# A graph kernel's passages between stages without a barrier, weights on another queue, and attention endings in six steps

## What is computed

```
h = relu(layernorm(x))
for W_r, W_sl, W_el in two layers:                       # "layer one", "layer two"
    self_msg = where(in_deg == 0, h @ W_el, h @ W_sl)
    agg = segment_sum((rel_embed[type] + h[src]) @ W_r, dst)
    h = rrelu(agg * deg ** -0.5 + self_msg)
x = x + h                                                # x2
h3 = relu(layernorm(x))
qk = h3 @ Wqk + bqk ;  v = h3 @ Wv + bv                  # attention over the same edges
e = exp(clip(qk[dst] . qk[src] / sqrt(D), -5, 5) - max)
out = segment_sum(e / sum(e) * v[src], dst) @ Wo + bo
x = x + gamma * layernorm(out + h3) + beta
```

## Time and profile before

| | us |
|---|---|
| median of 3 runs | 870.51 (868.87 to 872.46) |
| the profiled execution | 870.01 |
| its span, first to last instruction | 868.3 |
| PE busy | 732.6 (84%) |
| DVE busy | 527.7 (61%) |
| ACT busy | 431.5 (50%) |
| POOL busy | 245.1 (28%) |

### The profile page before, as it was taken

One profiled execution on the slowest core, in us unless ns is written; L12 is line 12 of the kernel. 1 busy time (PEld: TensorE's weight loads), 2 busy tenths in 40 slices (PEclk: granted clock), 3 DMA queues, 4 the chain that ended last, 5 costly groups with the idle time before them and its releaser, 6 DMA issues. The chain is left out here.

```text
span 868.3 us, 15380 instructions
## 1 busy us (share of the span) xinstructions
PE 732.6 (84%) x5767; PEld 545.2 (63%) x5767; DVE 527.7 (61%) x931; ACT 431.5 (50%) x1085; POOL 245.1 (28%) x273
## 2 busy tenths in 40 slices
PE   4266698898889898977399999859999999999993
PEld 3255587788778788866289999824444444444463
DVE  4987997786768677541033333414476767666676
ACT  0445765564555555551011111237767676767661
POOL 6130010000001111100000000026666666666662
PEclk9999799799989999987699999979999999999996
DMA  4100200033300000011311111130000000000000
GB/s 130 33 1 18 59 2 7 23 103 71 100 9 7 8 8 7 8 60 61 108 31 37 36 37 37 37 106 1 1 4 21 3 22 2 24 0 24 2 25 18
DMA packets 39763, 27.89 MB, mean 32 GB/s; under 512 B 5311, under 2 KB 38163, under 8 KB 39686
## 3 DMA queue, kind: packets, MB, share of 16 engines
q1 hardware_dynamic: 39206, 26.35, 10.5%
q10 hardware_dynamic: 480, 0.53, 0.2%
HBM read 13.28 MB, written 10.80 MB: 28 GB/s over the span
## 5 line engine op out<-in xcount | busy, mean ns | idle before, releaser
L1462 POOL TENSOR_TENSOR counts<-counts,work 125x500 f32<-125x500 f32 x150 | 162.3, 1082 | 97.5 <-DVE work L1526 84.1
L1016 PE MATMUL sums<-work 125*128 125x196 f16 (+15 forms) x1220 | 157.1, 256 | 24.7 <-DVE work L825 24.6
L1384 PE MATMUL a_ps_o<-work 125*128 125x500 f32 (+1 forms) x350 | 159.2, 545 | 7.1 <-DVE work L1530 6.7
L1526 DVE SCALAR_TENSOR_TENSOR work<-a_ps_s,counts 125x500 f32<-125x500 f32 x150 | 101.6, 677 | 93.5 <-ACT a_ps_s L1482 93.4
L1372 PE MATMUL a_ps_s<-work 128*125 128x500 f32 x300 | 152.0, 589 | 6.9 <-PEq L534 6.9
L819 DVE TENSOR_TENSOR work<-work,counts 125x3024 f16<-125x3024 f16 (+1 forms) x60 | 114.3, 1906 | 65.5 <-PE sums L1018 62.4
L1477 ACT ACTIVATE a_ps_s<-a_ps_s,work 125x500 f32<-125x500 f32 (+1 forms) x157 | 102.1, 650 | 86.5 <-PE a_ps_s L1372 83.4
L1018 PE MATMUL sums<-work 125*128 125x10 f16 (+15 forms) x800 | 133.7, 196 | 0.0
L1187 ACT CAST counts<-sums 128x364 f32 (+38 forms) x305 | 131.9, 472 | 2.1 <-issue 1.4
L977 PE MATMUL sums<-counts 125*128 125x250 f16 (+1 forms) x975 | 124.5, 275 | 10.0 <-ACT work L1129 10.0
L825 DVE TENSOR_TENSOR work<-work,counts 125x4200 f16<-125x4200 f16 (+15 forms) x120 | 125.5, 1086 | 0.0
(11 more groups left out here) (178 smaller groups left out, 703.3 us busy)
## 6 DMA issues: line engine op xcount, KB each, us to landing
first_columns<-counts SPq DMA_DIRECT2D x5, 610.4 KB
counts<-first_columns SPq DMA_DIRECT2D x5, 610.4 KB
counts<-counts SPq DMA_DIRECT2D x5, 468.8 KB
counts<-in_x SPq DMA_DIRECT2D x5, 312.5 KB
h_nodes<-counts SPq DMA_DIRECT2D x5, 312.5 KB
work<-in_x SPq DMA_DIRECT2D x12, 125.0 KB
x_after_messages<-work SPq DMA_DIRECT2D x12, 125.0 KB
h_attention<-work SPq DMA_DIRECT2D x12, 125.0 KB
```

What stands on the lines that cost most here:

```text
L1016: pe.matmul(win[:, 0:c, cols], lo[:, k * 2 * LO:k * 2 * LO + 128], m[:, k, h0 * w:(h0 + c) * w].rearrange("p (h d) -> p h d", d=w), start= ...
L1384: last = pe.matmul(ps_o[c % 2][:, 0:cols(u) // n], h3[:, j + i, :], pbuf[u % PB][:, i * NP:i * NP + cols(u) // n], start=j + i == 0, stop= ...
L1462: pool.tensor_tensor(a, a, p, ALU.add).then_inc(acc_done, 1)
L1526: dve.scalar_tensor_tensor(pbuf[u % PB], ps_s[u % 4][0:NP, 0:WIDE], float(np.exp(-CLIP)), counts[0:NP, j, c * WIDE:(c + 1) * WIDE], ALU.ma ...
```

## The change

It does the following.

1. **No block of its own for attention.** Its engines' programs become functions (dictionary `A`) which `messages` calls at the end of each engine's program. PSUM is one tensor of 8 banks for all. The first three scores start when `L["rows"]` says that 12 of 13 chunks of qk stand. What belongs to the last block (turn, copy, store of h3, qk, its row) is called as `last_turn`, `last_turned`, `last_qk`, `last_rows` at units 1 and 3 of attention.
2. **The tail of layer one and the head of layer two.** Chunk 11 has PSUM banks 2 and 3 and its own `ht`, and "own" of 11 comes ahead of "agg" of 10. ACT's and DVE's splits are interleaved piece by piece. The turn and the first 10 planes of layer two's first chunk are issued ahead of "agg" of chunk 12. The `hn` loads wait for 59 batches instead of 60.
3. **Weights.** Layer two's five weight loads and `x_last` move from SP to ACT's queue, behind its last split. The five heads loads move into layer two, one behind each of the first five chunks.
4. **Attention endings of six steps.** h3 + `bo` + `bvo`, and x2 + beta, are made ahead of the sums (`before`, three parts). Six parts remain: quotient plus what was made, stats, aggregate, normalize, gamma, plus x2 and beta. `final` waits for `var_done` instead of `y_ready`. The wv and wvo products come six units later.

```diff
+    banks1 = lambda c: (psum[:, 2, :], psum[:, 3, :]) if c == DIRECT + 1 else (psum[:, 6, :], psum[:, 7, :])
+    ht_of = lambda c: P["h_t2"] if c == DIRECT + 1 else ht
...
-            sp.wait_ge(ring_free, len(BATCHES))
+
+            sp.wait_ge(ring_free, len(BATCHES) - 1)
...
-            sp.wait_ge(sums_done, CHUNKS)
-            for i in range(5):
-                v = slice(5 * i, 5 * i + 5)
-                sp.dma_start(counts[0:NP, v, 0:HEAD], heads.rearrange("p (j d) -> p j d", d=HEAD)[:, v, :]).then_inc(heads_in, 16)
...
-            sp.wait_ge(agg_done, CHUNKS)
-            for t, v in zip((wr, ws[:, 0:D], ws[:, D:]), weights2):
-                sp.dma_start(t, v).then_inc(L["wts"], 16)
-            sp.dma_start(wqk, wqk_d).then_inc(L["wts"], 16)
...
+                if i < 5:
+                    v = slice(5 * i, 5 * i + 5)
+                    sp.dma_start(counts[0:NP, v, 0:HEAD], heads.rearrange("p (j d) -> p j d", d=HEAD)[:, v, :]).then_inc(heads_in, 16)
...
             ending(DIRECT)
+            split(0, 0)
             for i in range(4):
-                split(i)
-            split(4)
+                split(i + 1, 0)
+                split(i, 1)
+            split(4, 1)
             ending(DIRECT + 1)
...
+            for kind, c in (("own", DIRECT + 1), ("agg", DIRECT), ("sum", DIRECT + 1), ("self", DIRECT + 1),
+                            ("rest", DIRECT + 1), ("own", LAST), ("agg", DIRECT + 1), ("sum", LAST), ("self", LAST), ("rest", LAST)):
+                for step in by_kind.pop((kind, c)):
+                    layer1(*step)
+            assert list(by_kind) == [("agg", LAST)]
+            own(0, ORDER2[0])
+            sums(0, ORDER2[0], 0, EARLY).then_inc(early, 1)
+            layer1("agg", LAST, 0)
...
+            act.wait_ge(agg_done, CHUNKS)
+            for t, v in zip((wr, ws[:, 0:D], ws[:, D:]), weights2):
+                act.dma_start(t, v).then_inc(L["wts"], 16)
+            act.dma_start(wqk, wqk_d).then_inc(L["wts"], 16)
+            act.dma_start(bqk, bqk_d.rearrange("(p o) -> p o", o=1)).then_inc(L["wts"], 16)
+            act.dma_start(x_last, by_block(x, LAST)).then_inc(L["last_in"], 16)
...
+            pe.wait_ge(L["rows"], LAST)
+            A["tensor_first"](pe)
...
+    N_AT, F_AT, BEGIN_AT = 3, 4, 6
+    BEFORE_AT = ((3, 4, 5), (10, 11, 15))
+    ENDING_AT = ((7, 8, 9, 12, 13, 14), (16, 17, 18, 21, 22, 23))
+    ROOT_AT = (10, 19)
+    LAST_N, LAST_F = 0, 1
+
+    LAST_ENDING = ((), (), ((0, 0), (0, 1)), ((0, 2), (1, 0), (1, 1)), ((1, 2), (0, 3)), ((0, 4), (0, 5), (1, 3)), ((1, 4), (1, 5)))
...
+    def scalar_first(act):
+        act.wait_ge(consts, 2)
+        below(act, 0)
+        below(act, 1)
+        exponent(act, 0)
```

More of the change, by code:

```diff
@@ L620, in _ @@
             sp.wait_ge(L["x2_last"], 16)
+            sp.wait_ge(L["rows"], CHUNKS)
+            A["sync"](sp)
         @block.gpsimd
@@ new lines, in score @@
+    def score(pe, u):
+        c, j, n = units[u]
+        if u == NB - 1:
+            pe.wait_ge(T["rows"], -(-NB // 2))
+        out = ps_s[u % 4]
+        if c < FULL:
+            last = pe.matmul(out[0:NP, :WIDE], qk_t[:, j * NP:(j + 1) * NP], qk_t[:, c * WIDE:(c + 1) * WIDE], start=True, stop=True)
+        else:
+            for i in range(n):
+                last = pe.matmul(out[0:NP, i * NP:(i + 1) * NP], qk_t[:, (j + i) * NP:(j + i + 1) * NP], qk_t[:, FULL * WIDE:], start=True, stop=True)
+        last.then_inc(scores, 1)
@@ new lines, in below, with exponent @@
+    def below(act, u):
+        act.wait_ge(scores, u + 1)
+        s = ps_s[u % 4][0:NP, 0:cols(u)]
+        act.activation(s, s, ACT.Relu, bias=five, scale=-float(D) ** -0.5).then_inc(limited, 1)
+    def exponent(act, u):
+        act.wait_ge(limited, u + 1)
+        s = ps_s[u % 4][0:NP, 0:cols(u)]
+        act.activation(s, s, ACT.Exp, bias=five, scale=-1.0).then_inc(exped, 1)
+    def scalar_first(act):
[3 more added lines that the diff above has]
+        exponent(act, 0)
@@ new lines, in run_scalar, with take @@
+    def run_scalar(act, last_turned, last_rows):
+        def take(c):
+            act.wait_ge(pv_done, end_unit(c))
+            if c:
+                act.wait_ge(f_done, c)
+            w = blocks(c) * NP
+            act.copy(hv[:, 0:w], ps_o[c % 2][:, 0:w]).then_inc(hv_out, 1)
+        for u, (c, j, n) in enumerate(units):
+            if 0 < u < len(units) - 1:
+                below(act, u + 1)
+            if u:
+                exponent(act, u)
+            if u == 1:
+                last_turned()
+            if u == 3:
+                last_rows()
+            if c == 0 and j == 14:
+                act.wait_ge(wvo_done, 1)
+                act.copy(wv_t, ps_f[:, 0:D]).then_inc(wv_t_out, 1)
+            if c == 0 and j == 17:
+                act.wait_ge(wvo_done, 2)
+                act.copy(wvo, ps_f[:, D:2 * D]).then_inc(wvo_out, 1)
+                act.copy(bvo, ps_f[0:NP, 2 * D:3 * D]).then_inc(wvo_out, 1)
+            if 0 < c < FULL and j == 1 or c == FULL and j == 0:
+                take(c - 1)
+        take(FULL)
@@ L1400, in final @@
-            def final(c):
-                pe.wait_ge(hv_out, c + 1)
-                if c:
-                    for h, _ in halves(c - 1):
-                        pe.wait_ge(y_ready[h], c)
-                for b in range(blocks(c)):
-                    last = pe.matmul(ps_f[0:NP, b * D:(b + 1) * D], hv[:, b * NP:(b + 1) * NP], wvo, start=True, stop=True)
-                last.then_inc(f_done, 1)
-            for u in range(AHEAD):
-                score(u)
-            pe.wait_ge(consts, 2)
@@ new lines, in run_vector @@
+        for u, (c, j, n) in enumerate(units):
+            if u:
+                weigh(dve, u)
+            if c == 0 and j == 10:
+                dve.wait_ge(loaded, 16 * 6)
+                dve.tensor_copy(bv_w, bv_c.broadcast_to([D, NP])).then_inc(bvb, 1)
+            if 0 < c < FULL:
+                for h, m in halves(c - 1):
+                    if c == 1 and h == 0 and j == BEFORE_AT[0][0]:
+                        dve.wait_ge(wvo_out, 2)
+                    if j in BEFORE_AT[h]:
+                        before(c - 1, h, m, BEFORE_AT[h].index(j))
+                    if j == BEGIN_AT and h == 0:
+                        begin(c - 1)
+                    if j in ENDING_AT[h]:
+                        ending(c - 1, h, m, ENDING_AT[h].index(j))
+            if c == FULL:
+                k = j // AB
+                if k in (0, 1):
+                    for part in range(3):
+                        before(FULL - 1, k, 2, part)
+                if k == 2:
+                    begin(FULL - 1)
+                for h, part in LAST_ENDING[k]:
+                    ending(FULL - 1, h, 2, part)
```

610 lines of the change are left out of this document (304 added, 306 removed).

## The result

The changed kernel takes 839.17 us (median of 4 runs, 837.45 to 842.03) against 870.06 us before (4 runs, 868.87 to 872.46): a ratio of 0.9645, 95% interval 0.9611 to 0.9679. The profiled execution took 839.33 us with a span of 836.7; before it was 870.01 and 868.3.

What follows compares the result with a forecast made beforehand. PE was taken as the bound, busy throughout 584 to 837 us, so only the two passages and the end could gain. 23.7 + 6.6 - 0.5 + 5.0 = 34.8 us off 870.0 gave 835.2, stated as 835.5 us; range 828 to 845.

Steps and rivals of the forecast that it cites:

- The heads loads cost nothing where they go now.: Layer two's first five chunks: heads loads fit SP's queue behind the h3 stores, and h3 is needed only later; 0 us.
- The rival's price of up to 3.9 us a chunk: Layer two: if the cover were gone, heads loads would delay five chunks by up to 3.9 us each, 19 us.
- Passage one: Layer one to layer two: shorter waits and earlier weights bring `weigh` 22.7 us earlier; 23.7 us with 1.0 for clock.
- The clock behind the long wait: Layer two's first `weigh`: it ran at half clock behind PE's 15.1 us weights wait; a shorter wait gains 1.0 us.
- ACT becomes the late one: Layer one to layer two: ACT's six issues, table load and copy delay `weigh` to 412; time 841, chance 0.12.
- The weights still wait: Before layer two: weights wait for a queue or unseen traffic, leaving 4 us gain; 855; chance 0.06 with heads delays.
- What I had worked out from shared DMA engines: Before layer two: moving weights to ACT's queue alone leaves them among heads' packets; most of the 15.1 us stays.
- Its second form: Layer two: heads loads delay each of five chunks by their full 3.9 us; same 855, within the shared chance 0.06.
- Passage two: Layer two to attention: unit 0 starts 10.8 us earlier without the barrier, 4.1 given back; gain 6.6 us (3 to 10.5).
- the two stalls: Attention's first units: ACT waits for PE's last-block turn and product, delaying units 2 and 4; 4.1 us given back.
- The middle: Attention's long stretch stays bounded by PE; DVE's added steps lose 0.5 us (0 to 3).
- The end: Last attention endings: DVE work leaving the path gains 4.0 us before the last unit, 1.0 behind; 5.0 (3.5 to 6).

## Why the prediction came out as it did

The time lies in the range, 3.7 us above the point, but part of that is luck: a loss of 11.7 us that I had at nothing was covered by more gain elsewhere and, in the profiled execution, by 3.05 us of chance. By its steps:

- **The wrong step is "The heads loads cost nothing where they go now."** They cost 11.7 us in five chunks. I had looked at two things: that SP's queue has room in a chunk of 10.9 us, and that h3 is not needed soon. What is late is neither, but the next chunk's x load, issued 2.7 to 3.6 us behind the piece. The rival's price of up to 3.9 us a chunk named the right kind of loss; it was 1.7 to 3.0. PE lost 7.6 us in four waits, and the lowered clock around them fits the other 4.1 (`weigh` at 1.91 us for 1.03). Three other runs with the same code there had full clock in layer two and took 137.9 to 138.5 us. Moving the pieces gave back 8 to 10 us by which of these one compares with 129.9.
- **Passage one** gave 25.0 where I had 22.7. The starts of the sums and of chunk 12 were right to 1 us (chunk 12 at 389.2 on before's scale, forecast 389.8). Errors went against each other. ACT's last split ended 2.4 us earlier than forecast (400.1 on before's scale, forecast 402.5), and bqk was there at most 2.9 us after its issue began, where I had put 3.7 us from the issue's end on. ACT's six issues took 4.0 us and not 2.7, and PE's conditional block cost 2.0 us that I had at nothing.
- **The clock behind the long wait** was put at 1.0 us and is 2.9: I had priced the first `weigh` alone, and the weights' product, the turn and the whole set of sums behind it ran slow too.
- **The rival "ACT becomes the late one"** is true as a bound and not as a price: ACT is the last, by 0.34 us.
- **"The weights still wait"** fell in its first form: on either queue passage one is 33.6 to 33.7 us as long as the heads are elsewhere. What I had worked out from shared DMA engines, that on ACT's queue among the heads' packets most of the 15.1 us would stay, came out wrong too: with the heads in flight the wait was 2.2 us, and what was saved was lost at x. Its second form, the heads' delay of each of five chunks, is the one that came, at 11.7 us and not 19.
- **Passage two**: forecast 6.6, measured 7.35. Unit 0 came 5.94 us behind the row (forecast 6.2), and the two stalls gave back 3.7 us (forecast 4.1). Moving the two copies recovered 3.5 of these. No run kept the barrier alone, so that the 11 us of the earlier unit 0 are its removal is read from the trace.
- **The middle**: forecast -0.5, measured -0.1. It was 255.7 to 255.8 us in all runs that left attention's first units as they were.
- **The end**: forecast 5.0, measured 5.17, of which 2.85 were shown to be the biases' steps.
- Without the 3.05 us of chance the traces would be 28.6 us apart, 6.2 short of my sum: 11.7 by the heads, made up for by 1.9 of clock behind the wait, 2.3 in passage one and 1.3 in the three other stretches.

## What to carry to other kernels

When a large transfer is moved into another stage, ask which small load is issued next and whose packets it will follow; put the big piece behind the load that the chain needs, or cut it until its delay is less than the chain's slack. An issue queue with room in it says nothing about that. When a copy in an in-order stream waits for another engine, one place later can be enough, if the units around it can run ahead.

## What the runs showed of the hardware

- A piece of 610 KB kept the DMA share near 0.34 at about 118 GB/s. An x load of 125 KB issued behind it was used 6.4 to 7.3 us later when it stood on the same queue and 5.3 to 6.6 us when the piece was on ACT's; with no piece in front it was about 3.4.
- Issued on ACT's queue while SP's issued heads pieces for 21.3 us, bqk came 5.7 us after its issue (403.86 to 409.54); with none it was at most 2.9.
- PE's conditional block, not taken, cost 1.55 and 0.47 us of idle time around 24 matmuls, and these went with it. In the nine other traces with the block on this path the two were 1.3 to 2.2 us and 0.2 to 0.9 us.
- The granted clock of a stretch in which nothing had changed differed by execution (0.86 to 0.97 from 200 to 250 us), and the ring's end by up to 6.8 us. With 0.97 it came at 369.3 to 369.5 us (three profiles), with 0.90 to 0.92 at 370.5 to 374.2 (eight), but the three others (0.86 and 0.93, 367.4 to 371.3) do not follow this order, so that window alone does not give the ring's end. Differences below that are to be read from stretches, not from the whole time.
